# Block 1 of a four-block kernel: the sums with v of two steps in one TensorE run, in every second step

## The chip, the cores and the metric

The kernel runs on one core of one Trainium2 chip. What is measured is the time of one execution on the device, in microseconds (us). Kernels are compared by the median of several executions. The profile is of one further execution, taken by the hardware profiler, which records every instruction with its start and duration.

Engines are named as the profile names them: PE is TensorE (PEld its weight loads), DVE is VectorE, ACT is ScalarE, POOL is GpSimd, SP is SyncE, which only issues DMAs here.

## What is computed

The reference chains four blocks over 8 sequences of 512 tokens and 256 channels: an attention with 16 heads of 16 channels, a mixture of slots and experts, a retention layer, and two local-attention layers. The change touches the first one only. What it computes, cut to what matters:

```python
qkv = (x @ Wqkv).reshape(Bx, Nx, 3, H, HD).transpose(2, 0, 3, 1, 4)
q, k, v = (qkv[0], qkv[1], qkv[2])
attn = jnp.einsum('bhnd,bhmd->bhnm', q, k) * (SCALE / TEMPERATURE)
attn = attn * alpha[None, :, None, None] + beta[None, :, None, None]
attn = jax.nn.softmax(attn, axis=-1) * gamma[None, :, None, None]
...
enhanced_v = v * (1.0 + ka)
out = jnp.einsum('bhnm,bhmd->bhnd', attn, enhanced_v)
out = out.transpose(0, 2, 1, 3).reshape(Bx, Nx, Cx)
return out @ Wproj + bproj
```

The softmax is taken over 512 keys, for each of 8 x 16 (sequence, head) pairs.

## The kernel before

**Units and steps.** Block 1 handles four heads of one sequence as a unit: there are 32 units (`UNITS`), four to a sequence. A unit has four steps t = 0 to 3, one for each tile of 128 tokens, and a step handles one tile of all four heads (j = 0 to 3, `UNIT`). `tensor1`, `scalar1` and `vector1` each go through the same list of steps (u, t); nothing reorders the work at run time: each engine runs its own list, written out in Python, and waits on semaphores.

**Two products of q and k.** Each score tile of 128 x 512 is computed twice. Line 232 computes it with the queries on the partitions, two units ahead (`LAG`): DVE reduces it to one maximum for each query (line 481). Line 245 computes it with the keys on the partitions, from the same operands and with the (negated) maxima added as further rows; ACT takes its exponential (line 393) into `ex`. So for each j PE issues one matmul of line 232 and one of line 245. I call them M and X, with the number j: M0 X0 M1 X1 M2 X2 M3 X3 is a step.

**Banks and buffers.** M has three PSUM banks (`k % 3`): an M waits until the reduction of three M's ago is done (`a_m`). X has two banks (`exp_bank1`, banks 3 and 4): an X waits until the exponential of two X's ago is done (`a_e`). In the last two units, where no M's are left, X has all five banks. `ex` has three buffers, one for each step in turn: the exponentials of a step wait for the sums with v of three steps ago (`a_av`).

**The sums with v.** `tensor1_values` (lines 261 to 273) multiplies the exponentials of one step with v. It has four float32 matmuls (line 272), one for each head, each with 32 columns of weights and 512 columns of data; the four write four different groups of 32 partitions of bank 5 and run at the same time. The trace shows two records for each, so eight records for one step's sums. The four steps of a unit are accumulated in bank 5 (start at t = 0, stop at t = 3), and then DVE copies the bank out (line 517, `vector1_aside`), between M1's and M2's reduction in the first step of the next unit. Before the first of the four, the engine waits until all four exponentials of that step are done (`a_e` at 4k + 4). In the kernel before, the sums of a step stand in the next step, behind X1.

**Tasks.** Behind X3 of a step come tasks of that step (`tasks1`): projections to q and k ("qk", line 298) and to v ("v", line 304) of the next sequence, the shift rows of the next unit ("shift", line 310), the output projection of the sequence before ("proj", line 318) and its transposes ("turn0", "turn1", line 324). DVE and ACT have parts of them: DVE scales the sums ("scale", lines 547 and 550, after a DMA), adds the projection to x and takes its statistics (lines 555 and 557), normalises ("apply", line 2617), and prepares the shift rows after each t = 3 (lines 524 to 532).

## Time and profile before

| | us |
|---|---|
| three timed runs | 2338.45, 2332.77, 2335.21 |
| their median | 2335.21 |
| the profiled execution | 2338.43 |
| its span in the trace | 2336.6 |

Over the whole span PE is busy for 2245.0 us (96%), DVE for 1635.4 us (70%), ACT for 1254.6 us (54%) and POOL for 731.7 us (31%). Block 1's steps fill the trace from about 28 us to 554 us: 34 units of steps, the first two with M's alone and the last two with X's alone. The granted clock of PE there is 1.00 but for short stretches at the start.

A matmul's duration in the trace is longer than the distance to the next one, because matmuls overlap. What PE has spent is therefore read from the starts, not from the durations. An idle time of PEld says little in the same way: weights are loaded ahead, and nothing can be loaded ahead while the sums with v run.

### The profile page before, as it was taken

To read this page: it belongs to the slowest core of one execution; us is meant where nothing else is said; L and a number is where in the kernel's file an instruction comes from. 1 tells how busy PE (TensorE), PEld (TensorE's weight loads), DVE (VectorE), ACT (ScalarE), POOL (GpSimd) and SP (SyncE) were. 2 spreads that over 40 slices of the span, in tenths; PEclk is the share of its full clock that TensorE was granted. 3 is DMA by queue.
4 is the path that set the end of the run, shared out by engine and by line. 5 is a ranking of instruction groups with operands and counts; after the bars stand their busy time and mean duration, and the time that the engine had idled before them with its cause. 6 is when DMAs were issued, how large, how long until landed. Compare 5 with 4: busy or idle time off the path is not lost.

```text
span 2336.6 us, 42445 instructions
## 1 busy us (share of the span) xinstructions
PE 2245.0 (96%) x16257; PEld 1318.4 (56%) x16306; DVE 1635.4 (70%) x4252; ACT 1254.6 (54%) x2823; POOL 731.7 (31%) x730
## 2 busy tenths in 40 slices
PE   8999999999998999989899999999999999999998
PEld 3333333334633867756566666666666666666665
DVE  6788888886502846668786677677767777787763
ACT  4666666665221622247666656655655665566640
POOL 3343323321121411144433333333333333333321
PEclk7999999999998999999999999999999999999999
DMA  7454343335297020000000000000001000000001
GB/s 239 156 152 122 116 119 121 113 91 183 79 402 318 2 91 19 28 28 13 6 6 6 4 3 6 6 2 33 15 6 53 6 15 23 20 6 24 21 23 40
DMA packets 68617, 158.44 MB, mean 68 GB/s; under 512 B 6256, under 2 KB 49120, under 8 KB 63936
## 3 DMA queue, kind: packets, MB, share of 16 engines
q1 hardware_dynamic: 65856, 146.55, 17.8%
q0 software_dynamic: 2560, 9.18, 1.7%
q8 instruction: 130, 2.13, 0.4%
q14 instruction: 71, 0.58, 0.1%
HBM read 116.39 MB, written 35.13 MB: 65 GB/s over the span
## 4 chain that ended last, share of the span: by engine, by line
PE 74%; DVE 14%; ACT 4%; DMA 3%; issue 3%; POOL 1%; SPq 0%; another core or an unknown queue 0%; POOLq 0%; DVEq 0%; ACTq 0%
PE banks L2059 10%; PE banks L2037 7%; PE banks L1918 6%; PE banks L1932 5%; PE banks L232 4%; PE banks L272 4%; PE banks L2019 3%; PE banks L245 3%; PE banks L1962 3%; PE banks L1977 3%; DVE arena L481 2%; PE banks L1441 2%; PE banks L1944 2%; PE banks L298 2%; PE banks L2003 1%
## 5 line engine op out<-in xcount | busy, mean ns | idle before, releaser
L481 DVE TENSOR_REDUCE arena<-banks 128x1 f32<-128x512 f32 x512 | 322.8, 682 | 62.0 <-PE banks L232 61.1
L393 ACT ACTIVATE arena<-banks 128x512 f32<-128x512 f32 x512 | 280.3, 596 | 137.4 <-PE banks L245 113.3
L2059 PE MATMUL banks<-arena 128*128 128x512 f32 x640 | 293.2, 594 | 1.0 <-DVE arena L2244 1.0
L2141 ACT ACTIVATE arena<-arena 128x256 f32<-128x256 f32 (+1 forms) x512 | 286.6, 563 | 5.0 <-DVE arena L2250 4.5
L2397 POOL TENSOR_TENSOR arena<-arena 128x512 f32<-128x512 f32 x128 | 162.7, 1271 | 381.0 <-DVE arena L2281 381.0
L1918 PE MATMUL banks<-arena 128*128 128x512 f32 x512 | 241.5, 594 | 2.8 <-DVE arena L2281 2.8
L232 PE MATMUL banks<-arena 96*128 96x512 bf16 x512 | 203.3, 400 | 13.4 <-DVE arena L481 9.3
L2393 POOL TENSOR_TENSOR arena<-arena 128x16 f32<-128x16 f32 x64 | 189.3, 2958 | 5.4
L2113 ACT ACTIVATE arena<-arena 128x256 f32<-128x256 f32 (+1 forms) x256 | 102.1, 471 | 162.8 <-DVE arena L2226 162.8
L2059 PEld LDWEIGHTS banks<-arena 128*128 128x128 f32 x640 | 115.5, 190 | 126.7 <-issue 116.5
L245 PE MATMUL banks<-arena 128*128 128x512 bf16 x463 | 174.9, 383 | 3.1 <-ACT arena L393 2.2
L2037 PE MATMUL banks<-arena 128*128 128x256 f32 x768 | 171.1, 379 | 1.9 <-DVE arena L2337 1.9
L2244 DVE CUSTOM_DVE_ANT_0 arena<-banks,arena 128x256 f32<-128x256 f32 (+1 forms) x512 | 168.8, 386 | 3.5 <-PE banks L1962 3.5
L2037 PEld LDWEIGHTS banks<-arena 128*128 128x128 f32 x768 | 144.5, 190 | 28.0 <-issue 6.2
L232 PEld LDWEIGHTS banks<-arena 96*128 96x128 bf16 x512 | 50.1, 98 | 180.2 <-DVE arena L481 110.0
L1918 PEld LDWEIGHTS banks<-arena 128*128 128x128 f32 x512 | 91.5, 190 | 86.9 <-issue 81.3
L272 PE MATMUL banks<-arena 128*32 128x512 f32 x1024 | 136.9, 607 | 2.5 <-ACT arena L393 1.6
L2133 ACT ACTIVATE arena<-banks 128x512 f32<-128x512 f32 x64 | 38.2, 597 | 180.4 <-PE banks L1932 180.4
L2289 DVE TENSOR_TENSOR arena<-arena 128x512 f32<-128x512 f32 x64 | 81.9, 1279 | 73.5 <-POOL arena L2397 73.5
L1932 PE MATMUL banks<-arena 128*128 128x512 f32 x256 | 126.7, 617 | 0.3 <-ACT arena L2091 0.3
L2019 PE MATMUL banks<-arena 128*128 128x256 f32 x512 | 121.2, 380 | 0.0
L1977 PE MATMUL banks<-arena 128*128 128x128 f32 x896 | 119.7, 272 | 0.5 <-DVE arena L2244 0.3
(304 smaller groups left out, 4231.3 us busy)
## 6 DMA issues: line engine op xcount, KB each, us to landing
arena<-in_e_W SPq DMA_DIRECT2D x16, 2048.0 KB, 16.0
arena<-stacks SPq DMA_DIRECT2D x64, 384.0 KB, 4.6
arena<-in_e_Wg SPq DMA_DIRECT2D x8, 2048.0 KB, 16.8
stacks<-arena SPq DMA_DIRECT2D x32, 384.0 KB, 2.5
stacks<-arena SPq DMA_DIRECT2D x32, 256.0 KB, 2.8
arena<-dens POOLq DMA_DIRECT2D x32, 256.0 KB, 4.9
arena<-in_xT SPq DMA_DIRECT2D x8, 512.0 KB, 7.9
stacks<-arena SPq DMA_DIRECT2D x32, 128.0 KB, 2.6
```

The lines of the kernel that those rows point to most:

```text
L232: e.matmul(self.psum[:, k % 3], stack[0:STACK, 0, j, t * P:(t + 1) * P], stack[0:STACK, 1, j, :], start=True, stop=True).then_inc(s["a_max ...
L245: e.matmul(self.psum[:, self.exp_bank1(k)], stack[:, 1, j, t * P:(t + 1) * P], stack[:, 0, j, :], start=True, stop=True).then_inc(s["a_exp ...
L272: i = e.matmul(bank[32 * j:32 * j + 32, :], v[:, t, at:at + 32], ex[:, j], start=t == 0, stop=t == TILES - 1, skip_group_check=True)
L393: e.activation(ex[:, j], self.psum[:, self.exp_bank1(k)], ACT.Exp).then_inc(s["a_e"], 1)
L481: e.tensor_reduce(split(self.maxima[n % 2][:, 0:16], TILES, UNIT)[:, t, j:j + 1], self.psum[:, k % 3], AX.X, ALU.max, negate=True).then_in ...
L1918: k = e.matmul(self.psum[:, side], self.xT[:, b, c, at:at + P], self.wqkv4[:, c, side], start=c == 0, stop=c == 1)
L1932: k = e.matmul(self.psum[:, 2], self.xT[:, b, c, at:at + P], self.wqkv4[:, c, 2], start=c == 0, stop=c == 1)
L1977: k = e.transpose(bank[:, hh, n], pr[:, 2 * pair + hh, n * P:(n + 1) * P], self.ident)
L2019: k = e.matmul(self.psum[:, 2, 0:CH], self.o4[0][:, pair * P:(pair + 1) * P], self.wo4[:, pair], start=pair == 0, stop=pair == 3)
L2037: i = e.matmul(bank[:, t % 2 * CH:(t % 2 + 1) * CH], self.hidden[k][:, at:at + P], self.w2[:, k + t // 2 if last else k], start=k == 0, st ...
L2059: i = e.matmul(bank, weights[:, c], self.hT[:, c], start=c == 0, stop=c == 1)
L2141: k = e.activation(pr[:, h, at:], pr[:, h, at:], ACT.Exp, bias=mx[:, h:h + 1], scale=rn[:, h:h + 1], accum_out=den[:, h:h + 1])
```

## The change

The sums of a step no longer stand in the next step each. `before` becomes a list of steps whose sums are due. At j = 1 of the steps with t = 0 and t = 2 the list is worked off: the sums of the two latest steps in one run, eight matmuls instead of four. Steps with t = 1 and t = 3 have no sums. The last step of all, (31, 3), has a run for (31, 2) alone, and its own sums stand behind it, as before. Of 128 runs 63 double ones and two single ones are left. `tensor1_values`, the waits in it, all buffers and banks, and the lists of the other engines stay as they are.

```diff
-        before = None
+        before = []
         for u, t in self.steps1():
...
-                if j == 1 and before is not None:
-                    self.tensor1_values(e, w, *before)
-            before = (u, t) if u >= 0 else None
+                if j == 1 and (t % 2 == 0 or (u, t) == (UNITS - 1, TILES - 1)):
+                    for step in before:
+                        self.tensor1_values(e, w, *step)
+                    before = []
+            if u >= 0:
+                before.append((u, t))
...
-        self.tensor1_values(e, w, *before)
+        for step in before:
+            self.tensor1_values(e, w, *step)
```

All lines of the changed kernel behind this one have a number four higher: lines 272, 298, 318 and 324 are 276, 302, 322 and 328 there.

First place: PE's list from M1 of step (16, 3) to the sums in step (17, 0). Line 324 (328) is the task "turn1" behind X3 of (16, 3). Before:

```order
L232 MATMUL banks<-arena 128x512
L245 MATMUL banks<-arena 128x512
L272 MATMUL banks<-arena 32x512 x4
L232 MATMUL banks<-arena 128x512
L245 MATMUL banks<-arena 128x512
L232 MATMUL banks<-arena 128x512
L245 MATMUL banks<-arena 128x512
L324 MATMUL banks<-arena 128x128 x4
L232 MATMUL banks<-arena 128x512
L245 MATMUL banks<-arena 128x512
...
L272 MATMUL banks<-arena 32x512 x4
```

The same place now:

```order
L232 MATMUL banks<-arena 128x512
L245 MATMUL banks<-arena 128x512
L232 MATMUL banks<-arena 128x512
L245 MATMUL banks<-arena 128x512
L232 MATMUL banks<-arena 128x512
L245 MATMUL banks<-arena 128x512
L328 MATMUL banks<-arena 128x128 x4
L232 MATMUL banks<-arena 128x512
L245 MATMUL banks<-arena 128x512
...
L276 MATMUL banks<-arena 32x512 x8
```

The sums between X1 and M2 of (16, 3) are gone, and those of (17, 0) are of (16, 2) and (16, 3), eight matmuls in a row.

Second place: PE's list in the last two units, where there are X's alone, from the run in step (30, 0) on. Before:

```order
L272 MATMUL banks<-arena 32x512 x4
L245 MATMUL banks<-arena 128x512 x2
L310 MATMUL banks<-arena 32x128 x4
L245 MATMUL banks<-arena 128x512 x2
L272 MATMUL banks<-arena 32x512 x4
L245 MATMUL banks<-arena 128x512 x4
L272 MATMUL banks<-arena 32x512 x4
L245 MATMUL banks<-arena 128x512 x2
L318 MATMUL banks<-arena 128x256 x2
```

The same place now:

```order
L276 MATMUL banks<-arena 32x512 x8
L245 MATMUL banks<-arena 128x512 x6
L314 MATMUL banks<-arena 32x128 x4
L245 MATMUL banks<-arena 128x512 x2
L276 MATMUL banks<-arena 32x512 x8
L245 MATMUL banks<-arena 128x512 x6
L322 MATMUL banks<-arena 128x256 x2
```

Between two runs there are eight X's instead of four.

## Rows read from the trace of the kernel before

**Rows 1.** The page's costliest groups: lines of block 1 (columns as named there)

```profile
L481 DVE TENSOR_REDUCE arena<-banks 128x1 f32<-128x512 f32 x512 | 322.8, 682 | 62.0 <-PE banks L232 61.1
...
L232 PE MATMUL banks<-arena 96*128 96x512 bf16 x512 | 203.3, 400 | 13.4 <-DVE arena L481 9.3
...
L272 PE MATMUL banks<-arena 128*32 128x512 f32 x1024 | 136.9, 607 | 2.5 <-ACT arena L393 1.6
```

**Rows 2.** Busy time of the engines in two stretches: middle, and last two units

```profile
240.00:375.00 135.00, 131.62 (x679) 50.06 (x685) 116.64 (x225) 85.26 (x161) 42.06 (x52) 1.00 0.39 115
...
532.00:555.00 23.00, 20.99 (x123) 7.19 (x125) 10.05 (x26) 17.50 (x34) 0.00 (x0) 1.00 0.16 40
```

**Rows 3.** PE's timeline, one single run (start us, us, engine, line, count)

```profile
403.97 0.38 PE L245 MATMUL banks<-arena 128*128 128x512 bf16 x1
404.28 1.06 PE L272 MATMUL banks<-arena 128*32 128x512 f32 x8
405.28 0.39 PE L232 MATMUL banks<-arena 96*128 96x512 bf16 x1
```

**Rows 4.** PE's timeline in block 2: sixteen records of the same form, then others

```profile
672.77 1.92 PE L927 MATMUL banks<-arena 128*32 128x512 f32 x16
674.62 0.63 PE L929 MATMUL banks<-arena 16*32 16x512 f32 x4
```

**Rows 5.** PE's timeline, X2, X3 of step (16, 2), X0, X1 of (16, 3)

```profile
323.69 0.38 PE L245 MATMUL banks<-arena 128*128 128x512 bf16 x1
...
324.13 0.38 PE L245 MATMUL banks<-arena 128*128 128x512 bf16 x1
...
324.76 0.39 PE L245 MATMUL banks<-arena 128*128 128x512 bf16 x1
...
325.25 0.39 PE L245 MATMUL banks<-arena 128*128 128x512 bf16 x1
```

**Rows 6.** ACT's timeline, the four exponentials that belong to them

```profile
324.11 2.16 ACT L393 ACTIVATE arena<-banks 128x512 f32<-128x512 f32 x4 [0.83 <-PE banks L245]
```

**Rows 7.** PE's timeline, M0 and M3 of step (16, 1)

```profile
315.47 0.38 PE L232 MATMUL banks<-arena 96*128 96x512 bf16 x1
...
317.88 0.39 PE L232 MATMUL banks<-arena 96*128 96x512 bf16 x1
```

**Rows 8.** DVE's timeline around the end of "apply" before that step's reductions

```profile
316.52 0.70 DVE L2617 TENSOR_SCALAR arena<-arena 128x256 f32<-128x256 f32 x1
317.14 2.47 DVE L481 TENSOR_REDUCE arena<-banks 128x1 f32<-128x512 f32 x4
```

**Rows 9.** PE's timeline, M0 and M3 of step (18, 1)

```profile
346.84 0.38 PE L232 MATMUL banks<-arena 96*128 96x512 bf16 x1
...
350.10 0.39 PE L232 MATMUL banks<-arena 96*128 96x512 bf16 x1 [0.69 <-DVE arena L481]
```

**Rows 10.** DVE's timeline, "scale" before that step's reductions

```profile
347.01 1.42 DVE L547 SCALAR_TENSOR_TENSOR arena<-arena 128x512 f32<-128x512 f32 x2 [0.74 <-DMA arena<-dens]
...
349.37 1.28 DVE L481 TENSOR_REDUCE arena<-banks 128x1 f32<-128x512 f32 x2
```

**Rows 11.** DVE's timeline, "proj" between the reductions of (19, 2) and (19, 3)

```profile
371.62 0.42 DVE L555 TENSOR_TENSOR arena<-arena,banks 128x256 f32<-128x256 f32 x1 [0.23 <-PE banks L318]
372.08 0.43 DVE L557 BATCH_NORM_STATS2 arena<-arena 128x6 f32<-128x256 f32 x1
372.42 2.68 DVE L481 TENSOR_REDUCE arena<-banks 128x1 f32<-128x512 f32 x4
```

**Rows 12.** PE's timeline in the last two units, steps (30, 2) and (30, 3)

```profile
537.61 1.06 PE L272 MATMUL banks<-arena 128*32 128x512 f32 x8
538.61 1.04 PE L245 MATMUL banks<-arena 128*128 128x512 bf16 x4
540.17 1.07 PE L272 MATMUL banks<-arena 128*32 128x512 f32 x8 [0.53 <-ACT arena L393]
```

## The prediction

> **What bounds the kernel now.** I read the page's groups first, then the busy time by stretch, then timelines of PE, DVE and ACT side by side. Each of the 512 score tiles costs a matmul M (line 232), a matmul X (line 245), a reduction on DVE and an exponential on ACT; the sums with v are 1024 records in runs of eight, 128 runs [rows 1]. In the middle of block 1 PE is busy for 131.62 of 135 us and DVE for 116.64 [rows 2]. So PE is the bound, but DVE is at 86% and has only three banks of room, and ACT has only two. In the last two units DVE has little left to do (10.05 of 23 us), and PE is held back by ACT [rows 2, 12].
>
> **What the change takes off PE.** A single run starts 0.31 us behind the X ahead of it, and M2 follows 1.00 us behind the run's start [rows 3]. A plain X costs 0.22 us (X and M together 0.44 us [rows 5]), so the run takes 0.31 + 1.00 - 0.22 = 1.09 us from PE. What a double run costs, this trace shows in another block: sixteen records of exactly this form (128*32 weights, 512 float32 columns), then another matmul 1.85 us behind the start [rows 4]. So a double run takes 0.31 + 1.85 - 0.22 = 1.94 us, and two single ones 2.18 us: **0.24 us less for each of 63 pairs, 15.1 us** if nothing else moved.
>
> The Trainium skill, "TensorEngine Tiling (Array Packing)", section Key Properties, says that changing the tiling mode drains TensorE. That agrees with the lead of 0.31 us instead of 0.22 us and with the long tail of a run. By that rule alone the whole 15.1 us would come back.
>
> **What it costs: ACT's two banks.** Now a pair of steps is M0 X0 M1 X1, the long run, M2 X2 M3 X3, tasks, M0 X0 M1 X1 M2 X2 M3 X3, tasks. Each odd step (t = 1, 3) has four X's in a row with no run between them. What that does can be seen in (16, 2) and (16, 3), where no task stands between two steps: X2 at 323.69, X3 at 324.13, then X0 at 324.76 instead of 324.57, 1.07 us behind X2, because it waits for X2's exponential to leave the bank; the next X comes 0.49 us later instead of 0.44 [rows 5]. ACT takes 2.16 us for the four, back to back [rows 6]. So a chain of four costs 0.19 + 0.05 = 0.24 us. Before, only the steps without a task ahead of them paid that. A sequence in the middle has 16 steps, 8 pairs. In six of them a task stands between the even and the odd step, and the chain of four is new: +0.24 us, as much as the pair saves. In two (behind (4k, 2) and (4k + 2, 2)) no task stands there; they paid 0.24 us before and now have a chain of eight, about 0.35 us by the same two rates. They gain 0.24 - 0.11 = 0.13 us each, 0.26 us a sequence.
>
> **What it costs: DVE's three banks.** M3 of a step waits for the reduction of M0. Reductions follow each other in 0.60 us (four of them take 2.47 us [rows 8], one alone 0.68 us [rows 1]), start 0.42 us behind their M, as an exponential does behind its X (323.69 and 324.11 [rows 5, 6]), and PE goes on 0.73 us behind a reduction's start (349.37 and 350.10 [rows 9, 10]). In an odd step M3 now comes 1.55 us behind M0 (3 x 0.44, and 0.24 for ACT), so it is held as soon as DVE is late by more than 1.55 - 0.42 - 0.73 = 0.40 us; before, the single run gave 1.0 us more. By walking the eight pairs with these distances and the tasks' own from the rows I get:
> - (4k, 0) and (4k, 1), with "apply": DVE does M0's reduction at 317.14, 1.67 us behind M0 at 315.47 [rows 7, 8]. DVE's chain is unbroken from there back over two steps, so M3 at 317.88 can't come sooner, with any order of the runs. Gain 0, not 0.24.
> - (4k + 2, 0) and (4k + 2, 1), with "scale": M3 waits for the reduction at 349.37, and "scale" starts at 347.01 because of a DMA [rows 9, 10]. The longer run moves the reductions ahead of "scale" back to just behind that DMA: "scale" starts 0.1 us later. Loss 0.1.
> - (4k + 3, 0) to (4k + 3, 3), with "proj" between the steps: the reduction of M0 comes 0.80 us behind the start of the addition to x, which waits for the projection's last matmul [rows 11]. Before, this was hidden: M3 came 2.4 us behind M0. Now M0's reduction is done about 1.8 us behind M0, 0.2 us after M3 could go. Loss 0.05 and 0.18.
> - The 0.17 us by which the last of these sends DVE late into the next "apply" is lost again there.
>
> Together 0.5 us lost and 0.26 us gained, **0.24 us lost for each of the six middle sequences, 1.4 us**. In the first sequence and the eighth most even steps have no task behind them: four pairs of about 0.2 us and three of 0.15 to 0.3 us, **a gain of 1.5 us**.
>
> **The last two units.** From run to run it is 2.56 us here: M's are gone, and each run waits for the exponential of the X two places ahead of it (idle 0.53 us, until ACT [rows 12]). With a double run the first four matmuls belong to a step whose exponentials are long done, and only the second four wait. Eight X's stand between runs; the sixth exponential ends 0.42 + 5 x 0.48 + 0.60 = 3.42 us behind the first X (0.49 us apart in rows 6, 0.60 us long), and the X behind the run follows 1.0 us later: about 4.5 us for two steps instead of 5.12. Four such stretches (4.5 + 4.5 + 4.85 with a "proj" + 3.69 to the single run in (31, 3)) are 17.5 us, against 18.7 us before: **a gain of 1.2 us**.
>
> **The sum.** 15.1 us off PE's own list, and nearly all of it given back in waits: -1.4 + 1.5 + 1.2 = 1.3 us gained. The profiled execution took 2338.4 us (span 2336.6 us), 3.2 us above the median of 2335.2 us; by the median it is 2335.2 - 1.3 = 2333.9, **2334 us**. Covers that I rely on: `ex` has three buffers, and the exponentials of an odd step need the sums of two steps ahead of its even one, which the first half of the long run delivers some 2 us earlier; the copy of bank 5 (line 517) stands behind the run at t = 0 as before; the first sums of a unit now start at t = 2, so their wait for that copy is farther away, not nearer. No DMA, queue or list of another engine moves.
>
> **Rivals.**
> *A, the whole saving stays.* ACT and DVE catch up during the long run and the waits don't add up. 2335.2 - 15.1 = 2320 us; with half the waits 2328 us. For it: the rate of X's over a pair of steps is no higher than before. Against it: the banks are two and three whatever the mean rate is, and rows 5 show the wait in just this pattern.
> *B, slower: DVE runs late in every pair.* During the long run DVE gets nothing for 2.4 us and has at most 1.8 us of work in its banks. If its tasks (117 of 135 us busy) then leave it more than 0.40 us late at the odd step in all pairs, not only in those four, each pair loses what the pairs with "proj" lose, 0.15 us on average: 63 x 0.15 = 9.5 us, 2344 us. It decides from a lateness of 0.40 us at M0. The rows with "v" between the steps speak against it: there DVE has no task of its own.
> *C, the change doesn't do what it says.* The second four matmuls don't follow the first at the pace of rows 4, since they start again on the same partitions of the same bank, and a double run costs 2.0 us or more. Then only the waits are left: 45 chains of 0.24 us, 11 us slower, 2346 us. Against it: in rows 4, too, all sixteen records go to one bank, onto the same partitions.
>
> **Chances.** My forecast, within 2.5 us of 2334, and what lies around it out to the bound: 0.60. A with its half-way forms 0.25. B 0.10, C 0.05. A measurement of this kernel can tell about 0.2% (4.7 us) from no change. So faster by more 0.25, within it 0.60, slower 0.15. The errors of my walk are some 0.1 us a pair, 6 us over 63 pairs, both ways; to leave out no more than 2 in 10 the range goes from 2327 us (half of A) to 2341 us (more than half of B).
>
> **What would show it.** Right: in the trace after, a double run is followed 1.85 us behind its start; in odd steps X2 comes 1.07 us behind X0 and the wait is for line 393; PE's idle time ahead of lines 232 and 245 grows by about as much as the runs shrink; in the last two units runs of eight are 4.5 us apart. M3 of (16, 1) stays about 7.5 us behind M0 of (16, 0). Wrong: X2 0.88 us behind X0 in most odd steps (then A), or M3 held for line 481 by more than 0.3 us also in pairs with "v" (then B), or more than 1.9 us behind a double run's start (then C).

## The result, and the profile after

| | before | after |
|---|---|---|
| median, us | 2338.29 (13 runs, 2332.77 to 2341.71) | 2345.70 (13 runs, 2341.18 to 2351.49) |
| ratio of after to before, with a 95% interval | | 1.0031 [1.0022, 1.0039] |
| the profiled execution, us | 2338.43, span 2336.6 | 2348.96, span 2347.1 |

The changed kernel is **slower**, by 0.31%, where I forecast 2334 us and no change to speak of. The base itself moved by 3.1 us: the three runs that I started from had a median of 2335.2 us, thirteen have 2338.3. Beside that base the loss is 7.4 us by the medians and 10.5 us by the spans.

The page of the kernel after, its span, its engines and the groups of block 1 that answer to [rows 1] (line 481 is now 485, line 272 is 276; columns as there):

```profile
span 2347.1 us, 42446 instructions
...
PE 2245.4 (96%) x16259; PEld 1326.0 (56%) x16306; DVE 1636.2 (70%) x4252; ACT 1254.6 (53%) x2823; POOL 732.9 (31%) x730
...
L485 DVE TENSOR_REDUCE arena<-banks 128x1 f32<-128x512 f32 x512 | 319.3, 680 | 68.8 <-PE banks L232 68.6
...
L232 PE MATMUL banks<-arena 96*128 96x512 bf16 x512 | 203.3, 400 | 21.8 <-DVE arena L485 17.2
...
L276 PE MATMUL banks<-arena 128*32 128x512 f32 x1024 | 123.7, 599 | 0.4
```

The runs take 13.2 us less of PE (136.9 to 123.7), and PE's wait for reductions is up by 8 us (9.3 to 17.2). PE's sum is the same as before (2245.4 against 2245.0 us): part of what the runs gave back has probably gone into matmuls that run longer behind long waits, as shown below; no run separates that part.

**Where the time is.** I measured from the start of one run with v to the start of the next double run, so that both kernels are cut at the same place, (u, 0) or (u, 2). A pair's number in the table is the time from its run to the next one's.

| pair of steps | before | after | difference |
|---|---|---|---|
| (8,0) with "apply" | 11.12 | 10.93 | -0.19 |
| (8,2) | 6.38 | 6.35 | -0.03 |
| (9,0) | 6.98 | 7.00 | +0.02 |
| (9,2) | 7.42 | 7.43 | +0.01 |
| (10,0) with "scale" | 9.65 | 10.24 | +0.59 |
| (10,2) | 7.15 | 6.78 | -0.37 |
| (11,0) with "proj" | 8.11 | 8.13 | +0.02 |
| (11,2) with "proj" | 7.42 | 7.61 | +0.19 |
| **sequence of units 8 to 11** | 64.23 | 64.47 | **+0.24** |
| (6,0) with "scale" | 10.17 | 16.16 | +5.99 |
| (18,0) with "scale" | 10.51 | 14.88 | +4.38 |
| (26,0) with "scale" | 10.19 | 15.90 | +5.71 |
| (5,0) | 11.31 | 9.20 | -2.11 |
| (2,2) | 8.43 | 7.53 | -0.90 |

Units 12 to 15 read the same as units 8 to 11 to 0.02 us; in units 20 to 23 one pair, (20, 2), is 0.34 us longer than before. At the last run, in (31, 3), the kernel after is 13.1 us behind (564.35 against 551.22 us from the span's start); 2.6 us of that are given back behind block 1. **Three pairs, all of them with "scale", hold 16.1 us**; everything else in block 1 together gains 3.0 us, 0.8 of it ahead of the first run with v.

This table, and those like it below, read one execution of each kernel. The executions of one kernel differ by some 10 us, and the profiled one of the kernel after lies 3.3 us above its median. So the 16.1 us are where that execution lost its time; that each of the others has all three pairs as long isn't shown.

**The run costs what the prediction said.** This is PE's timeline of the kernel after, step (18, 0) and the next (start us, us, engine, line, count), the place of [rows 9]:

```profile
346.16 1.92 PE L276 MATMUL banks<-arena 128*32 128x512 f32 x16
348.02 0.82 PE L232 MATMUL banks<-arena 96*128 96x512 bf16 x2
...
351.49 0.38 PE L232 MATMUL banks<-arena 96*128 96x512 bf16 x1
352.05 0.39 PE L245 MATMUL banks<-arena 128*128 128x512 bf16 x1 [0.18 <-ACT arena L397]
355.95 0.61 PE L232 MATMUL banks<-arena 96*128 96x512 bf16 x1 [3.52 <-DVE arena L485]
356.36 0.63 PE L245 MATMUL banks<-arena 128*128 128x512 bf16 x1
356.92 0.61 PE L314 MATMUL banks<-arena 128*32 128x128 bf16 x4
357.45 2.79 PE L302 MATMUL banks<-arena 128*128 128x512 f32 x4
```

M2 follows 1.86 us behind the run's start (346.16 to 348.02); I had taken 1.85 from [rows 4]. The Trainium skill, "TensorEngine Tiling (Array Packing)", section Key Properties, ties a drain to the change of mode; the trace agrees in that with half as many changes 13.2 us of runs are gone. Below it the same rows show the loss: M3 of (18, 1) waits 3.52 us for a reduction, where it waited 0.69 us in [rows 9].

Behind that wait the matmuls take 0.61 us where they took 0.38, and the four of "qk" 2.79, where they took 1.99 in the kernel before. The granted clock says why. Busy time by stretch, kernel after (us, PE, PEld, DVE, ACT, POOL, each with its count, then the granted clock and the DMAs):

```profile
346.00:352.00 6.00, 5.82 (x30) 1.97 (x29) 3.33 (x7) 3.19 (x7) 0.43 (x1) 1.00 0.88 211
352.00:360.00 8.00, 4.44 (x11) 1.69 (x12) 7.67 (x10) 2.19 (x4) 4.08 (x4) 0.79 0.32 111
360.00:366.00 6.00, 5.86 (x33) 1.70 (x33) 3.96 (x7) 4.03 (x8) 3.54 (x4) 1.00 0.08 27
...
488.00:496.00 8.00, 6.64 (x15) 2.26 (x15) 5.92 (x10) 2.18 (x4) 2.87 (x4) 0.57 0.31 107
```

A clock of 0.79 over 8 us is half speed (1.2 instead of 2.4 GHz) for 3.4 of them: from 355.7 to 359.1 us. What PE did before it fell was to stand still, at 352.44 to 355.95. The Trainium skill, "TensorE: Matmul & The Clock Gate", section "HAM oscillation — how this bites in real kernels", describes just that: a wait lets the clock fall, and the work behind it starts slow. The trace agrees in all three places of the kernel after: M3 waits 4.75, 3.52 and 3.00 us, and half speed follows from 157.7 to 161.1, 355.7 to 359.1 and 488.8 to 495.6 us. The kernel before has one such stretch in this part of block 1, at 136.9 to 140.3 us in unit 5, behind a wait of PE of 2.54 us; the kernel after has none there, and gains 2.11 us at (5, 0). Not all of that is the clock: in e5 and e15 below, which have single runs there and no half speed, the pair takes 9.64 and 9.77 us, against 9.20 in the kernel after.

**What M3 waits for.** DVE's timeline of the kernel after, to be laid beside [rows 10]:

```profile
348.76 1.28 DVE L485 TENSOR_REDUCE arena<-banks 128x1 f32<-128x512 f32 x2
351.88 2.40 DVE L551 SCALAR_TENSOR_TENSOR arena<-arena 128x512 f32<-128x512 f32 x2 [1.84 <-DMA arena<-dens]
354.31 0.98 DVE L554 TENSOR_TENSOR arena<-arena 128x512 f32<-128x512 f32 x1
355.22 2.47 DVE L485 TENSOR_REDUCE arena<-banks 128x1 f32<-128x512 f32 x4
```

The reductions behind "scale" start at 355.22, M3 0.73 us later: the distance of [rows 9, 10], unchanged. But "scale" starts 5.72 us behind the run's start (351.88 - 346.16) instead of 3.76 (347.01 - 343.25), and its two operations take 2.40 us instead of 1.42. So M3 comes 1.96 + 0.98 = 2.94 us later behind the run, and the slow clock makes 1.45 us more before the next run: 4.39 us, against 4.38 measured.

Both sizes have a row. POOL's timeline of the kernel after: the issue of the reciprocals' store and their four loads (`dens`), and then POOL's share of the q and k stacks:

```profile
339.11 0.58 POOL L687 DMA_DIRECT2D dens<-arena  x1 [6.86 <-DVE arena L544]
342.74 1.97 POOL L690 DMA_DIRECT2D arena<-dens  x4 [3.05 <-DMA dens<-arena]
351.57 0.61 POOL L596 CAST arena<-arena 128x512 bf16<-128x512 f32 x1 [6.87 <-ACT arena L424]
352.26 1.47 POOL L598 TENSOR_TENSOR arena<-arena 128x512 f32<-128x512 f32 x1
```

SP's, the two loads of the next unit's stacks (384 KB each by the page), of the kernel after and then of the kernel before, and POOL's loads of the kernel before:

```profile
344.53 0.77 SPq L749 DMA_DIRECT2D arena<-stacks  x2
```

```profile
341.61 0.77 SPq L745 DMA_DIRECT2D arena<-stacks  x2
```

```profile
339.37 1.97 POOL L686 DMA_DIRECT2D arena<-dens  x4 [2.77 <-DMA dens<-arena]
```

Before, the last of the four small loads was issued at 340.85 us and the big ones stood 0.76 us behind it; "scale" could start 6.2 us behind that last issue. After, the last was issued at 344.21, the big ones 0.32 us behind it, and "scale" started 7.7 us behind. Against the run with v the big loads are issued where they were (1.64 and 1.63 us ahead of it), and the small ones 0.45 us later (2.40 us ahead of it before, 1.95 now): 0.45 later issued and 1.51 longer on the way make the 1.96 us. The 0.45 us come from the small store ahead of them (`dens<-arena`), which they wait for: it is issued 0.17 us later against the run (7.05 instead of 7.22 us ahead of it) and takes 0.28 us longer to land (3.35 instead of 3.07).

The other sequences bear the 1.51 us out. From its issue to its landing the last of the four small loads takes 5.4 to 6.1 us wherever the first big one stands 0.7 us or more behind it (units 10, 14, 18, 22 and 26 before, 10, 14 and 22 after), and 7.65 and 7.20 us in units 18 and 26 after, with 0.3 us between. Unit 6 is apart: 8.7 us after, with 0.96 us between, and 7.1 before, with 2.07.

When "scale" runs late it also runs beside POOL's CAST and TENSOR_TENSOR, which start at 351.57. The Trainium skill, "SBUF — State Buffer", section "SBUF: two separate sides", has a rule for that: an operation of VectorE with two inputs in SBUF and one of GpSimd that reads SBUF shut each other out, and the one that starts first goes first. "scale" has two such inputs. The traces agree: its pair takes 1.41 us when POOL is still (in e11, below), and 1.8 to 2.7 us in the three long pairs, where POOL's CAST or TENSOR_TENSOR is running when one of the two operations starts. In the kernel before, POOL's CAST starts at 347.79 us, behind the start of the second operation of "scale" in [rows 10]: there the pair keeps its 1.42 us, and it is the CAST that takes 1.10 us instead of 0.61.

**The last two units.** PE's timeline of the kernel after, the double run in step (30, 2), next to [rows 12]:

```profile
550.29 2.21 PE L276 MATMUL banks<-arena 128*32 128x512 f32 x16
552.66 0.59 PE L245 MATMUL banks<-arena 128*128 128x512 bf16 x2 [0.16 <-issue]
```

The four stretches are 4.23, 5.54, 4.55 and 3.98 us long, 18.30 in all against 18.74 before. This run holds its second half back for an exponential: the next X comes 2.37 us behind its start instead of 1.86. The run in (31, 2) does the same.

### The profile page after: what moved, and what is told of

Its sections match the earlier page's. It is cut to its first block, busy times and chain, and to the rows that moved or that the text cites. A ratio compares the mean times of both kernels' runs of the same rounds, so it can differ in the third digit from the quotient of the medians.

```text
span 2347.1 us, 42446 instructions
## 1 busy us (share of the span) xinstructions
PE 2245.4 (96%) x16259; PEld 1326.0 (56%) x16306; DVE 1636.2 (70%) x4252; ACT 1254.6 (53%) x2823; POOL 732.9 (31%) x730
## 4 chain that ended last, share of the span: by engine, by line
PE 69%; DVE 18%; ACT 4%; DMA 4%; issue 3%; POOL 2%; SPq 0%; another core or an unknown queue 0%; POOLq 0%; DVEq 0%; ACTq 0%
PE banks L2063 10%; PE banks L2041 7%; PE banks L1922 6%; DVE arena L485 5%; PE banks L1936 5%; PE banks L2023 3%; PE banks L1966 3%; PE banks L1981 3%; PE banks L276 3%; PE banks L232 3%; PE banks L245 2%; PE banks L1445 2%; PE banks L1948 2%; DMA arena<-in_e_Wg 2%; PE banks L2007 1%
## 5 line engine op out<-in xcount | busy, mean ns | idle before, releaser
L232 PE MATMUL banks<-arena 96*128 96x512 bf16 x512 | 203.3, 400 | 21.8 <-DVE arena L485 17.2
L276 PE MATMUL banks<-arena 128*32 128x512 f32 x1024 | 123.7, 599 | 0.4
```

What stands on the lines that cost most here:

```text
L232: e.matmul(self.psum[:, k % 3], stack[0:STACK, 0, j, t * P:(t + 1) * P], stack[0:STACK, 1, j, :], start=True, stop=True).then_inc(s["a_max ...
L276: i = e.matmul(bank[32 * j:32 * j + 32, :], v[:, t, at:at + 32], ex[:, j], start=t == 0, stop=t == TILES - 1, skip_group_check=True)
```

## Experiments

In all of these the ratio is to the kernel before, in runs on the same chip; its median was 2339.2 to 2340.5 us there, but for the last pair (2338.5). Lines are named by number in each kernel. Two explanations of the three long pairs stood against each other at first: the step (4k + 2, 1), which has lost its own run, so that its M's come closer together while "scale" runs; or what stands ahead of that step, the double run at (4k + 2, 0) included, which moves the loads of the reciprocals and those of the stacks against each other.

### The step beside "scale" alone, and all but it

e4 is the change with that step's run put back: in units 4k + 2 every step has a run again. The one at (4k + 2, 0) stays double.

```diff
-                if j == 1 and (t % 2 == 0 or (u, t) == (UNITS - 1, TILES - 1)):
+                if j == 1 and (t % 2 == 0 or u % 4 == 2 or (u, t) == (UNITS - 1, TILES - 1)):
```

> The changed kernel, but with single runs in the unit of scale: in steps (4k+2, 1) to (4k+3, 0) each step has the sums of the one before it; double runs everywhere else. If it is the missing run in (4k+2, 1) that turns a late scale into a long stall (theory R: PE arrives early, stands still, loses its clock): the three long stretches shrink by 3 us or more each, ratio 0.999 to 1.001. If it is what stands ahead, in unit 4k+1, that makes dens land late against DVE's arrival (theory D): the stretches stay at least 2 us over those of the kernel before, ratio 1.001 to 1.003.

Measured: 2355.42 us (2347.6 to 2363.49), 1.0074 [1.005, 1.0098]. The long pairs are there with the run back in them: (6, 0) is 6.1 us longer than before, (18, 0) 3.58, (26, 0) 2.37. So what stands ahead is enough. Another 5.5 us go in units 2 and 3, with half speed at 94.7 to 98.1 and 108.3 to 115.1 us; I have no explanation for those, so its total is no measure of anything.

e5 is the other half: single runs all over, but none in (4k + 2, 1), whose place is taken by a double one at (4k + 2, 2):

```diff
-                if j == 1 and (t % 2 == 0 or (u, t) == (UNITS - 1, TILES - 1)):
+                if j == 1 and not (u % 4 == 2 and t == 1):
```

> The kernel before with one double run in each sequence: the sums of (4k+2, 0) are taken out of (4k+2, 1) and stand with those of (4k+2, 1) in (4k+2, 2). Everything ahead of scale keeps the timing of the kernel before. Theory R: stalls of 3.9 us or more ahead of M3 of (4k+2, 1) in three sequences, as in the changed kernel, ratio 1.002 to 1.005. Theory D: dens land as in the kernel before, M3 waits at most 1.9 us, and the time stays within 0.1% of the kernel before.

Measured: 2341.74 us (2336.03 to 2349.81), 1.0015 [1.000, 1.003]. (18, 0) is 0.48 us shorter than before and (18, 2) 0.86 longer, with no long wait. DVE's timeline of e5 at (18, 1) and at (6, 1):

```profile
347.87 1.42 DVE L551 SCALAR_TENSOR_TENSOR arena<-arena 128x512 f32<-128x512 f32 x2 [0.27 <-DMA arena<-dens]
```

```profile
151.26 1.76 DVE L551 SCALAR_TENSOR_TENSOR arena<-arena 128x512 f32<-128x512 f32 x2 [1.09 <-DMA arena<-dens]
```

In unit 18 the missing run alone costs 0.38 us for the two pairs together. In unit 6 it costs 3.24 us, with a wait of 1.09 us for `dens` and half speed from 156.1 to 159.5 us. The two kernels together say that the lists ahead of "scale" decide in units 18 and 26, and that in unit 6 either of the two is enough.

### The stack loads issued later: two edits that failed

If the big loads delay the small ones, issuing them later should help. e1 is the kernel after, e2 the kernel before, with

```diff
-            if t == 0 and u >= 1 and u + 3 < UNITS:
+            if t == 1 and u >= 1 and u + 3 < UNITS:
                 self.fetch1(e, w, u + 3)
```

> The changed kernel with one edit: SP issues the loads of the next stacks (fetch1, 2 x 384 KB) one step later, at t = 1 instead of t = 0 of a unit. Theory D (the loads of the reciprocals, dens, land late because the stack loads are issued 0.3 to 1.0 us behind them and share the DMA engines; DVE then starts scale late, and PE stands still): the three long stretches from (6,0), (18,0) and (26,0), 14.9 to 16.2 us where 10.2 is usual, go back to 10.2 to 10.9 us, and the time falls by 12 to 16 us below the changed kernel, to 0.997 to 0.999 of the kernel before. Rival P (scale is slow because POOL cuts q and k into parts at the same time, and PE's clock then falls): scale still takes 3.3 to 4.3 us there, the stretches stay over 13 us, ratio 1.002 to 1.004.

> The kernel before with the same edit of SP's loads alone (fetch1 at t = 1). Theory D: its own small waits for dens go (three stretches of 10.2 to 11.3 us where 9.65 is usual), 1 to 3 us less than the kernel before, ratio 0.999 to 1.000. If it gains as much as the changed kernel does by the edit (over 8 us), the stack loads cost both kernels the same and D doesn't explain the difference between them.

and e6 (after) and e7 (before) have `t == 2` in that line.

> The changed kernel with fetch1 two steps later (t = 2 of a unit instead of t = 0), so that it is neither behind the dens loads nor, as at t = 1, ahead of the shift rows in SP's queue. Theory D (the stack loads share the DMA engines with the dens loads and make them land late): (18,0) to (18,2) and (26,0) to (26,2) take 10.2 us instead of 14.9 and 15.8, no half-speed stretch of PE's clock near them, ratio to the kernel before 0.997 to 1.000. Rival (dens land late by themselves): the two stay over 13 us, ratio 1.002 to 1.004.

> The kernel before with fetch1 at t = 2, the control to the one ahead. Theory D: 1 to 3 us less than before (its short waits for dens go), ratio 0.998 to 1.000. If it gains as much as the changed kernel does by the same edit, the loads cost both the same.

Measured: e1 2390.97 us (2385.43 to 2394.05), 1.0222 [1.0199, 1.0245]; e2 2373.68 (2371.73 to 2375.21), 1.015 [1.0129, 1.0171]; e6 2478.49 (2475.44 to 2482.38), 1.0598 [1.058, 1.0616]; e7 2471.54 (2467.34 to 2474.27), 1.0566 [1.0547, 1.0585]. All four are far slower, and not for the reason under study. PE's waits over block 1 (us in total, times, longest), of e1 and then of e6:

```profile
PE banks L245 <- DMA arena<-shifts: 21.7, 12, 3.4
PE banks L232 <- DMA arena<-stacks: 13.4, 11, 2.8
```

```profile
PEld banks L232 <- DMA arena<-stacks: 97.3, 18, 11.4
...
PE banks L232 <- DMA arena<-stacks: 91.2, 18, 11.1
```

SP works its list in order. One step later the loads stand behind the stores of the q and k stacks, whose wait is for POOL, and at t = 2 behind more of them; the M's then wait for their operands, and in e1 the X's for their shift rows, which come through the same queue. I had moved the loads past waits of the same queue without pricing them. One thing can be read in spite of that: with the loads out of the way, (18, 0) and (26, 0) of e2 fall from 10.51 and 10.19 us to 9.65, and those of e1 are 10.24 and 10.23, with no wait for `dens`. (6, 0) of e1 is still 4.9 us too long, with 1.4 us of it.

### "scale" one step later: another that failed

e3 (after) and e8 (before) give the reciprocals a step more:

```diff
-            at[4 * k + 2, 0].append(("scale", b, 0))
-            at[4 * k + 2, 1].append(("scale", b, 1))
+            at[4 * k + 2, 1].append(("scale", b, 0))
+            at[4 * k + 2, 2].append(("scale", b, 1))
```

> The changed kernel with both halves of scale one step later, behind (4k+2, 1) and (4k+2, 2). DVE comes to it 3 to 4 us later, when dens have landed. Theory L (the loss of the change is DVE waiting for dens, with PE still and its clock halved behind it, in three sequences): no wait for dens, unit 4k+2 takes about 17 us in every sequence, as it does now in the good ones, ratio 0.996 to 1.000. Rival W (what is lost is the sum of the small waits on ACT's and DVE's banks, 0.1 to 0.2 us a pair): ratio stays at 1.002 to 1.004.

> The kernel before with scale one step later, the control to the one ahead. Theory L: its own waits there are 0.5 to 1.1 us in three sequences, so 1 to 3 us less, ratio 0.998 to 1.000, and the changed kernel with this edit comes within 2 us of it.

Measured: e3 2358.55 us (2356.3 to 2360.18), 1.0084 [1.007, 1.0099]; e8 2354.42 (2349.63 to 2356.26), 1.0063 [1.0047, 1.0079]. One wait for `dens` is left in block 1 of each (0.8 and 1.0 us), and both are slower all the same: "scale" now stands at a place where PE has no tasks to cover it and where POOL is at work. DVE's timeline of e8:

```profile
366.88 2.31 DVE L547 SCALAR_TENSOR_TENSOR arena<-arena 128x512 f32<-128x512 f32 x2
```

There it takes 2.31 us for its pair without a wait for any DMA, while POOL's CAST starts at 366.33 and its TENSOR_TENSOR at 367.02 us. So it is what runs on POOL, not late data, that goes with a slow "scale", and the new place costs 1.7 to 6.7 us at (4k + 2, 2). Between the two kernels 4.1 us remain; the waits that cause them are not those of the kernel after, so this pair doesn't decide.

### "scale" without its data

e9 (after) and e10 (before) leave the reciprocals out: "scale" multiplies the sums by themselves instead of by `dens`, and waits for the loads only in the last sequence. The softmax's division is missing from both. All instructions and all DMAs stay.

```diff
-            w.wait_ge("a_inv_l", 64 * (unit + 1))
+            if unit == SEQS - 1:
+                w.wait_ge("a_inv_l", 64 * (unit + 1))
...
-                ..., self.factor[:, 2 * index + g, unit:unit + 1], self.dens[:, cols[g]],
+                ..., self.factor[:, 2 * index + g, unit:unit + 1], sums[:, cols[g]],
```

> The changed kernel with scale reading the sums themselves instead of dens (the division by the softmax's denominators is left out for sequences 0 to 7, so the output is another), and no wait for dens but for the last sequence. All DMAs are still issued. Theory L (the change loses by DVE's wait for dens in three sequences, and what follows from it): no long stretch at (6,0), (18,0) and (26,0), 10.2 us each as in the good sequences; ratio 0.996 to 1.000 to the kernel before. Rival W (the small waits on banks): the time stays at 1.002 to 1.004.

> The kernel before with the same edit (scale reads the sums instead of dens, the division by the denominators left out, no wait for dens but for the last sequence). Theory L: its own waits there go, 1 to 3 us, ratio 0.998 to 1.000, and it stands within 2 us of the changed kernel with this edit, on either side. Rival W: it is 6 us or more faster than the changed kernel with this edit.

Measured: e9 2335.72 us (2333.4 to 2337.95), 0.9982 [0.9973, 0.9991]; e10 2335.45 (2332.08 to 2336.9), 0.9979 [0.9968, 0.999]. **Without the wait for the reciprocals the change makes no difference.** From after to e9 10.0 us are gone, from before to e10 3.8 us. All three long pairs are gone with them: (6, 0), (18, 0) and (26, 0) take 10.24 to 10.28 us in e9 and 9.65 in e10. A middle sequence (units 8 to 27) takes 64.45 or 64.46 us in e9, but for one of 65.12 whose pair (20, 2) takes 7.02 instead of 6.35, and 64.21 to 64.23 in e10: the 0.24 us that the prediction has. Outside these sequences the profiled executions owe part of their likeness to chance: e10 has a stretch at half speed in unit 5, where (5, 0) takes 11.30 us against 9.07 in e9, and e9 has one from 509.5 to 512.9 us, where (28, 0) takes 10.26 us against 8.56 in e10. And the difference inside the pair is the plain part of the surprise: 10.24 - 9.65 = 0.59 us where the double run stands ahead of "scale", with no DMA in it, of which the next pair gives 0.37 us back (6.78 instead of 7.15). "scale" starts 3.80 us behind the run's start there, instead of 2.94, as the double run takes 0.86 us more.

PE's wait for reductions, us in total, times, longest, of after, before and e9:

```profile
PE banks L232 <- DVE arena L485: 16.4, 10, 4.8
```

```profile
PE banks L232 <- DVE arena L481: 8.5, 16, 2.5
```

```profile
PE banks L232 <- DVE arena L485: 6.0, 10, 1.8
```

### The stack loads held until the reciprocals are in

e9 takes the wait away but says nothing of why the data came late. e11 (after) and e12 (before) keep the whole computation and let SP hold the big loads of units 4k + 2 until the small ones have landed:

```diff
             if t == 0 and u >= 1 and u + 3 < UNITS:
+                if u % 4 == 2 and u >= 6:
+                    w.wait_ge("a_inv_l", 64 * (u // 4))
                 self.fetch1(e, w, u + 3)
```

> The changed kernel with one wait more: SP holds the stack loads of step (4k+2, 0) (k = 1 to 6) back until dens have landed, at the same place of its queue. Theory D (these loads make dens land late): DVE's wait for dens at (6,0), (18,0) and (26,0), 1.4 to 2.2 us, falls below 0.5 us, the long stretches go back to 10.2 to 10.9 us, ratio 0.996 to 1.000. Rival (dens land late for a reason of their own, such as the 0.6 us more that the store ahead of them takes): the waits stay over 1 us, ratio 1.002 to 1.004.

> The kernel before with the same wait in SP's queue. Theory D: the waits for dens of 0.4 to 0.7 us in three sequences go, ratio 0.998 to 1.000; if it comes out at or below the changed kernel with this wait, it is the best version so far.

Measured: e11 2337.94 us (2333.19 to 2341.18), 0.9991 [0.9982, 1.0]; e12 2336.65 (2333.1 to 2340.62), 0.9988 [0.998, 0.9997]. e11 is 7.8 us faster than the kernel after, and (18, 0) and (26, 0) take 10.35 and 10.24 us. DVE's timeline of e11 at (18, 1), the same operations as in the kernel after, and M3 on PE's:

```profile
350.12 1.28 DVE L485 TENSOR_REDUCE arena<-banks 128x1 f32<-128x512 f32 x2
351.42 1.41 DVE L551 SCALAR_TENSOR_TENSOR arena<-arena 128x512 f32<-128x512 f32 x2
352.87 0.69 DVE L554 TENSOR_TENSOR arena<-arena 128x512 f32<-128x512 f32 x1
```

```profile
354.22 0.39 PE L232 MATMUL banks<-arena 96*128 96x512 bf16 x1 [0.42 <-DVE arena L485]
```

"scale" starts right behind the reductions, without a wait, and POOL's work begins at 352.93, when it is done: 1.41 us again. DVE's waits for the reciprocals over units 6 to 31, of after, e11 and before:

```profile
DVE arena L551 <- DMA arena<-dens: 6.3, 4, 2.2
```

```profile
DVE arena L551 <- DMA arena<-dens: 2.1, 2, 1.5
```

```profile
DVE arena L547 <- DMA arena<-dens: 2.6, 4, 1.0
```

So in units 18 and 26 it is the big loads, issued so close behind, that delay the small ones: with the big ones held the last small one lands 5.94 and 5.42 us behind its issue, instead of 7.65 and 7.20. In unit 6 it isn't, or not they alone: (6, 0) still takes 15.70 us, with 1.45 us of waiting for `dens` and half speed from 156.5 to 163.3 us. **Why the reciprocals land late there stays open.** One DMA stands there and in no later unit with "scale": SP's load of 512 KB of x (`in_x`, the last but one of eight). In the kernel after SP issues it at 142.70 us and POOL the four small loads from 142.81 on (144.70 and 145.22 in the kernel before). The last of the small ones takes 8.0 us to land in e11, and 7.0 in e12, with no big load behind it. No run moves that load, so it is a candidate and no more. The medians of e11 and e12 are 1.3 us apart where their spans are 5.2, so (6, 0) can hardly be as long in every execution of e11.

### What PE's saving is worth

Rival A said that the 15.1 us could stay. Where they go can be shown by making ACT's and DVE's queues shorter. e13 is e11, e14 is e12, with the exponential of the first 256 of 512 columns alone (the other half of `ex` is left as it was):

```diff
-                    e.activation(ex[:, j], self.psum[:, self.exp_bank1(k)], ACT.Exp)
+                    e.activation(ex[:, j, 0:TOKENS // 2], self.psum[:, self.exp_bank1(k), 0:TOKENS // 2], ACT.Exp)
```

> The changed kernel with the stack loads held back behind dens (as e11), and with exponentials of the first 256 of each 512 columns only (the other half of ex keeps what stood there, so the output is another): an exponential then takes about 0.33 us instead of 0.60. Theory B (the 15 us taken off PE's list are given back because X waits for ACT's two banks in each chain of four): X two places on comes 0.42 + 0.33 + 0.05 = 0.80 us behind, under the 0.88 us of the list, so the chain's 0.24 us are gone in all pairs that DVE doesn't hold, and this kernel is 5 to 9 us faster than the single-run kernel with the same edits. Rival V (DVE's three banks hold the pairs anyway): within 2 us of the single-run kernel with the same edits.

> The kernel before with the stack loads held back behind dens (as e12) and the same short exponentials. Theory B: here only chains of four without a task between them wait, two in a sequence of 16 steps, so the edit brings 3 to 6 us at most (with the last two units, which wait for ACT), and it stays 5 to 9 us above the double-run kernel with the same edits. Rival V: within 2 us of it.

Measured: e13 2337.79 us (2333.47 to 2343.1), 0.9987 [0.9975, 0.9999]; e14 2331.98 (2330.26 to 2334.18), 0.9959 [0.9947, 0.9972]. Chains of four X's no longer stall, and yet nothing comes back: in units 8 to 15 the pairs gain 0.2 to 0.3 us a sequence on the single runs (63.82 and 63.83 against 64.13 and 64.00), and in units 16 to 27 two of three sequences of e13 are 0.3 and 0.5 us longer, the third 0.1 us shorter. PE's timeline of e13:

```profile
303.33 0.39 PE L232 MATMUL banks<-arena 96*128 96x512 bf16 x1 [0.37 <-DVE arena L485]
```

Now M3 waits for DVE instead of X2 for ACT. PEld's waits in a stretch of 80 us in the middle (240 to 320) say the same; of after and then of e13:

```profile
PEld banks L245 <- ACT arena L397: 8.0, 17, 0.7
```

```profile
PEld banks L232 <- DVE arena L485: 9.8, 22, 0.8
...
PEld banks L245 <- ACT arena L397: 3.7, 11, 0.5
```

In the total e13 is slower than e14 by 5.8 us. In the profiled executions the long pair at (6, 0), which is there again (17.57 against 10.21 us), is the largest part of it.

e16 is e9 and e17 is e10 with this edit and with half the reduction, too; the division, half the exponentials and half of each maximum are left out in both:

```diff
-                    e.tensor_reduce(..., self.psum[:, k % 3], AX.X, ALU.max, negate=True)
+                    e.tensor_reduce(..., self.psum[:, k % 3, 0:TOKENS // 2], AX.X, ALU.max, negate=True)
```

> The changed kernel without dens in scale and without the wait for them (as e9), and with both the exponentials and the reductions to the maxima over the first 256 of 512 columns only (division, half of the exponentials and half of each maximum are left out, so the output is another). A reduction then takes about 0.42 us instead of 0.68, an exponential 0.38 instead of 0.60. Theory T (PE's list is 0.24 us shorter for each pair, and it was the two queues behind it, first ACT's banks, then DVE's, that took it back): with both eased, this kernel is 9 to 14 us faster than the single form with the same edits. Rival N (the double runs save PE nothing, or something else holds it): within 3 us of the single form.

> The kernel before with the same edits as e16. Theory T: 9 to 14 us above e16, itself 8 to 14 us under the kernel before. Rival N: within 3 us of e16.

Measured: e16 2309.61 us (2307.95 to 2310.87), 0.9869 [0.9844, 0.9894]; e17 2318.11 (2316.05 to 2319.55), 0.9903 [0.9881, 0.9924]. **With both queues short the change gains 8.5 us** (9.8 by the spans). Of the spans' gain 4.4 us lie in the pair (5, 0) alone, where e17 runs at half speed from 133.5 to 136.9 us. The undisturbed middle sequences are the cleaner measure: 1.23 us each in three of five (61.51 against 62.74), of the 8 x 0.24 = 1.9 us that PE's list has; the other two of e16 take 63.12 and 61.71 us. Busy time in 60 us of the middle, of e16, e17 and after:

```profile
240.00:300.00 60.00, 59.74 (x323) 24.19 (x322) 41.90 (x106) 29.40 (x75) 20.37 (x26) 1.00 0.44 129
```

```profile
240.00:300.00 60.00, 59.83 (x315) 22.98 (x314) 40.12 (x104) 29.31 (x74) 20.29 (x26) 1.00 0.43 129
```

```profile
240.00:300.00 60.00, 58.39 (x303) 22.97 (x312) 51.17 (x101) 38.32 (x73) 21.34 (x26) 1.00 0.39 116
```

PE is full in both, and the one with double runs gets 323 records through in it, the other 315; in the kernel after DVE is busy for 51.17 us of the 60 and PE stands for 1.6.

### A version that keeps the gain at the end

e15 leaves nothing out. It is e11 with double runs in the last four units alone. Of these only unit 30 has a "scale", and no M is left there to wait behind it:

```diff
-                if j == 1 and (t % 2 == 0 or (u, t) == (UNITS - 1, TILES - 1)):
+                if j == 1 and (u < 28 or t % 2 == 0 or (u, t) == (UNITS - 1, TILES - 1)):
```

> The kernel before with the stack loads held back behind dens (as e12), and double runs in units 28 to 31 only, where no dens and few tasks stand between the steps. The pairs there saved about 1 us in the changed kernel: 0.5 to 1.5 us under e12, ratio to the kernel before 0.998 to 0.999. If the double runs were worth nothing there, it equals e12.

Measured: 2336.55 us (2334.76 to 2338.28), 0.998 [0.9972, 0.9989]. It beats both kernels, and so does e12 (0.9988 [0.998, 0.9997]), from which it can't be told. In its profiled execution (28, 0) takes 10.12 us instead of 8.56, with half speed from 512.1 to 515.5 us, which is more than the double runs behind it gain. What is worth having here is the held load, not the double run.

## Why the prediction was wrong, point by point

- **What the runs take off PE: right.** 1.86 us behind a double run's start for a forecast 1.85; 13.2 us of busy time fewer. Rival C is out. In e16 and e17, where PE is full, 1.23 of the 1.9 us a sequence come through.
- **ACT's two banks: right.** X2 was to come 1.07 us behind X0 in odd steps and the next X 0.49 us later. PE's timeline of the kernel after, X0, X2 and X3 of (17, 1):

```profile
335.55 0.38 PE L245 MATMUL banks<-arena 128*128 128x512 bf16 x1
...
336.62 0.39 PE L245 MATMUL banks<-arena 128*128 128x512 bf16 x1
...
337.10 0.39 PE L245 MATMUL banks<-arena 128*128 128x512 bf16 x1
```

  1.07 and 0.48 us. Rival A fails on this. That the wait is small in the page's group (3.8 us for line 245) only shows that the weight loads take it up.
- **DVE's banks: right in sum, but by errors that cancel.** I had +0.24 us for a middle sequence, and it is +0.24 (e9 against e10, and units 8 to 15 of the two kernels). That the two agree to the last digit is luck: the term of "scale" was 0.5 us too small, and those of "apply" and of (4k + 2, 2) made it up. "apply" was put at a gain of 0, and a loss of 0.17 for the lateness that "proj" sends into it, and gains 0.19 us; the "proj" pairs at losses of 0.05 and 0.18 and have 0.02 and 0.19. M3 of (16, 1) is 7.3 us behind M0 of (16, 0), for 7.5. The walk had 0.26 us of gain at (4k, 2) and (4k + 2, 2), of which 0.03 came at the first; at the second the 0.37 us belong to "scale". Rival B isn't what made the loss: the pairs with "v" between their steps differ by 0.02 us. e13 shows its mechanism once ACT no longer comes first.
- **The pair with "scale": the step that failed.** The prediction says that "scale" starts 0.1 us later, because the reductions fall back to just behind the DMA, and that "no DMA, queue or list of another engine moves". The lists don't move, but their times do. First, in sequences without a wait for `dens` the reductions ahead of "scale" decide, and there a double run costs 0.59 us, of which 0.37 come back. I had read one sequence of eight, (18, 0), and it is one of those that wait for the DMA. Second, and larger: I held the landing of the reciprocals fixed. It hangs on the loads issued near them (e11), and the change brings the two 0.45 us closer. In (18, 0) "scale" was 1.96 us late for a forecast 0.1; POOL's work made it 0.98 us longer; the clock fell behind the wait and cost 1.45 us. The sum of such places is 16.1 us, where the forecast had 0.1 each. The cause is shown for units 18 and 26, 10.1 of the 16.1 us; in unit 6 the landing moved too, but what moved it stays open.
- **First and eighth sequence: near in size, by luck.** 1.5 us forecast, 1.2 measured. Units 0 to 3 gain 1.0 us from the first run on, 0.9 of it at (2, 2), and units 28 and 29 0.2. I had 0.15 to 0.3 us for each of seven pairs; but for (2, 2) and (29, 0), none gains more than 0.14, and four lose. Why (2, 2) gains 0.9 no run shows. The 2.11 us at (5, 0), a stretch at half speed that is gone, weren't foreseen.
- **The last two units:** 1.2 us forecast, 0.44 measured. The stretches of 4.5, 4.5, 4.85 and 3.69 us were 4.23, 4.55, 5.54 and 3.98 (in time the 5.54 comes second). Not one but three of them hold an output projection. The one of (30, 2) is 0.7 us longer than I had it, and two of the four double runs wait in their middle for an exponential, 0.5 us each. I had put the exponentials 0.49 us apart "in rows 6", but four in 2.16 us with 0.60 for one are 0.52 apart.
- **The base:** 3.1 us of the miss of 11.7 are the median of three runs that it started from.

What made the loss is the pair with "scale" and its wait of 0.74 us, which the forecast treated as a fixed date; with that wait out of both kernels the two are level (2335.7 us for e9, 2335.5 for e10), for a forecast gain of 1.3. What isn't explained: the late landing in unit 6, the pair (20, 2), and the 5.5 us of e4 in units 2 and 3.

## What to carry to other kernels

A wait of a few tenths for a DMA, on the path and repeated, is a warning: any shift of the lists around it changes which transfers travel together, and the landing must be given a range of its own, from the slowest instance of that wait and not from one sample. Read such a place in every repetition before costing it. Where two engines each have a queue just long enough, taking work off a third can give nothing: here shortening one of them (e13) only moved the wait to the other, and with both short (e16) it paid. That the reductions alone wouldn't have been enough was not tried. And what is worth trying here first was to order the urgent small load ahead of the big one by a wait, which costs one line. But moving the big load to a later place in a queue that works in order cost far more here than it could bring.

## What the runs showed of the hardware that I had not expected

- In unit 18 four loads of reciprocals (256 KB each by the page) took 6.2 us from the last issue to use with two loads of 384 KB issued 0.76 us behind them, and 7.7 us with 0.32 us between. With those held back there was no wait.
- Two SCALAR_TENSOR_TENSOR on 128x512 float32 took 1.41 us alone (e11), 1.42 us where POOL's CAST started behind them, and 2.40 us where it had started first; 2.31 us in e8, with no wait for a DMA.
- A PE that had stood still for 3.5 us went on at half speed for 3.4 us: M 0.61 instead of 0.38 us, four "qk" matmuls 2.79 instead of 1.99.
- Two runs of four column groups back to back cost 1.86 us and one 1.00: the second four cost 0.86.
